# A four-layer block on one core: Delta net's gate moved from VectorE to ScalarE, the rope sum read from PSUM, and two chains of stages spread by one unit

## The reference, cut to what matters

```
q, k, v = x @ Wq, x @ Wk, x @ Wv
q, k = rope(q), rope(k)                      # u1*c - u2*s, u1*s + u2*c
q, k = elu(q) + 1, elu(k) + 1
beta = clip(sigmoid(x @ Wbeta + bbeta), 0.001, 0.999)
M = M * beta_t + k_t v_t^T ;  Z = Z * beta_t + k_t    # over the 1024 positions
y = (q_t M) / (q_t Z + eps)
```

## Time and profile before

| | |
|---|---|
| median of 3 runs | 1531.02 us (1529.54 to 1532.64) |
| profiled execution | 1541.69 us |
| its span | 1540.3 us |
| PE busy | 1185.7 us (77%) |
| DVE busy | 1129.7 us (73%) |
| ACT busy | 734.5 us (48%) |
| POOL busy | 704.0 us (46%) |
| mean granted clock of TensorE | 0.878 |

### The profile page before, as it was taken

One profiled execution on the slowest core, in us unless ns is written; L12 is line 12 of the kernel. 1 busy time (PEld: TensorE's weight loads), 2 busy tenths in 40 slices (PEclk: granted clock), 3 DMA queues, 4 the chain that ended last, 5 costly groups with the idle time before them and its releaser, 6 DMA issues.

```text
span 1540.3 us, 18685 instructions
## 1 busy us (share of the span) xinstructions
PE 1185.7 (77%) x5568; PEld 543.4 (35%) x5568; DVE 1129.7 (73%) x3003; ACT 734.5 (48%) x1599; POOL 704.0 (46%) x857
## 2 busy tenths in 40 slices
PE   3514986999998886657658678898989898988863
PEld 1212454555444443223222222333333333333322
DVE  5888645757988898578959786787888788876022
ACT  4634783255443253123230366656565656565641
POOL 7434672456777776438550122133412441335144
PEclk9856998999999996687875698999999999999995
DMA  3000104222111100004235101111020202000010
GB/s 107 0 1 0 46 1 108 80 77 62 35 48 42 35 14 0 0 4 63 43 51 78 20 1 30 32 17 35 4 33 15 37 4 33 4 1 3 1 42 14
DMA packets 33666, 47.02 MB, mean 31 GB/s; under 512 B 5007, under 2 KB 18191, under 8 KB 33263
## 3 DMA queue, kind: packets, MB, share of 16 engines
q1 hardware_dynamic: 30974, 43.84, 13.4%
q10 hardware_dynamic: 2592, 2.00, 0.5%
HBM read 39.14 MB, written 6.68 MB: 30 GB/s over the span
## 4 chain that ended last, share of the span: by engine, by line
PE 31%; DVE 21%; ACT 6%; issue 4%; POOL 4%; DMA 0%; ACTq 0%; DVEq 0%; POOLq 0%
PE PS L658 8%; PE PS L616 5%; PE PS L641 5%; DVE PS L1175 4%; DVE SS L1178 4%; PE PS L703 3%; DVE RB L1090 2%; PE PS L501 2%; PE PS L310 2%; ACT RB L1580 2%; DVE st L745 1%; ACT RB L1587 1%; DVE B L1090 1%; DVE PS L1070 1%; PE PS L520 1%
## 5 line engine op out<-in xcount | busy, mean ns | idle before, releaser
L1580 ACT ACTIVATE RB<-PS 128x512 f32<-128x512 f32 (+3 forms) x768 | 328.1, 497 | 265.7 <-PE PS L641 261.8
L616 PE MATMUL PS<-B 96*128 96x512 bf16 (+3 forms) x768 | 259.1, 360 | 55.6 <-DVE B L1221 24.2
L1829 POOL TENSOR_SCALAR_AFFINE_SELECT RB<-RB 128x512 f32<-128x512 f32 x128 | 81.3, 635 | 410.8 <-ACT RB L1580 410.8
L1175 DVE CUSTOM_DVE_ANT_0 PS<-PS,w_msk 128x128 f32<-128x128 f32 (+3 forms) x512 | 243.4, 503 | 29.1 <-PE PS L616 28.6
L641 PE MATMUL PS<-B 96*128 96x512 bf16 (+3 forms) x768 | 241.5, 336 | 18.6 <-ACT RB L1580 16.8
L1178 DVE TENSOR_REDUCE SS<-PS 128x1 f32<-128x512 f32 x256 | 175.2, 684 | 37.0 <-PE PS L616 36.1
L658 PE MATMUL PS<-RB,B 128*32 128x512 f32 (+3 forms) x1536 | 170.8, 517 | 14.4 <-ACT RB L1587 14.4
L616 PEld LDWEIGHTS PS<-B 96*128 96x128 bf16 x768 | 77.0, 101 | 204.8 <-DVE SS L1175 65.5
L1748 POOL TENSOR_TENSOR RB<-RB,B 128x512 f32<-128x512 f32 x64 | 82.6, 1292 | 92.9 <-DVE RB L983 68.1
L501 PE MATMUL PS<-B,WW 128*128 128x512 f32 x128 | 82.2, 776 | 37.6 <-DVE RB L1090 26.6
L641 PEld LDWEIGHTS PS<-B 96*128 96x128 bf16 x768 | 75.6, 100 | 99.1 <-ACT RB L1580 59.3
(11 more groups left out here) (243 smaller groups left out, 2229.3 us busy)
## 6 DMA issues: line engine op xcount, KB each, us to landing
B<-scrW SPq DMA_DIRECT2D x128, 128.0 KB, 3.0
B<-scrQ SPq DMA_DIRECT2D x72, 128.0 KB
scrQ<-B SPq DMA_DIRECT2D x6, 384.0 KB, 6.4
B<-scrK SPq DMA_DIRECT2D x36, 64.0 KB
X<-in_x SPq DMA_DIRECT2D x8, 256.0 KB, 8.5
out_dram<-X SPq DMA_DIRECT2D x8, 256.0 KB, 3.0
B<-in_w SPq DMA_DIRECT2D x3, 576.0 KB, 4.8
B<-in_zeros SPq DMA_DIRECT2D x9, 128.0 KB
```

The source lines that it names most:

```text
L616: pe.matmul(p[:, 0:w], qs[u % 3][:, h, 128 * i:128 * i + 128], keys_of(u, h)[:, 512 * c:512 * c + w], start=True, stop=True).then_inc(s["m ...
L1175: ins = dve.tensor_tensor_reduce(p, p, msk[:, 512 - w:512], 1.0, LOWEST, ALU.add, ALU.max, MX[:, u % 2, i, h, c:c + 1])
L1580: act.activation(RB[:, 4 * (step % 3) + z, 0:w], bank(bank_of["score", step, z])[:, 0:w], ACT.Exp).then_inc(s["ex2"], 1)
L1829: pool.affine_select(out=pb, in_=pb, compare_op=ALU.is_ge, fill=0.0, base=0, pattern=[[0, 4], [1, 128]], channel_multiplier=-1).then_inc(s ...
```

## The change

The gate 0.5 tanh + 0.5, clipped to 0.001..0.999, was two DVE operations on 128x512. It becomes three on ACT, each waiting for the one before: relu(0.5 t + 0.499), relu(0.998 - that), 0.999 - that. They stand in slices 12 and 13 ahead of the tanh of slice 12. The rope's second product is written back into its own PSUM bank, and the sum reads it there; the bank is lent until the sum is made. ACT's exp and relu go from slices 8, 10 to 9, 11 and DVE's elu from 9, 11 to 10, 12. `stats_m` goes from v-3 to v-4, `rstd` from v-4 to v-5, `add_m` and `add` from v-5 to v-6. POOL does what lies between units for the first unit of a step ahead of the product of the second.

```diff
@@ tensor_program, head_d
-                    banks.lend(i, s["t_d"], 4 * g + k - 6)
+                    w, half = divmod(k - 7, 2)
+                    if half:
+                        banks.lend(i, s["rot_d"], 2 * g + w + 1)
+                    else:
+                        banks.lend(i, s["t_d"], 4 * g + k - 6)
@@ vector_program, head_d
-                    dve.tensor_tensor(row(q + half), bank(bank_of["pj_d", g, k - 7]),
-                                      cs[:, half, 512 * h:512 * h + 512], ALU.mult).then_inc(s["t_d"], 1)
+                    p = bank(bank_of["pj_d", g, k - 7])
+                    dve.tensor_tensor(p if half else row(q), p, cs[:, half, 512 * h:512 * h + 512],
+                                      ALU.mult).then_inc(s["t_d"], 1)
                     if half:
                         dve.wait_ge(s["t_d"], 4 * g + k - 6)
-                        dve.tensor_tensor(row(q), row(q), row(q + 1), ALU.add).then_inc(s["rot_d"], 1)
-                if k in (9, 11):
-                    w = (k - 9) // 2
+                        dve.tensor_tensor(row(q), p, row(q), ALU.add).then_inc(s["rot_d"], 1)
+                if k in (10, 12):
+                    w = (k - 10) // 2
...
-                if k in (12, 13):
-                    d = BETA[k - 12][:, 512 * g:512 * g + 512]
-                    dve.wait_ge(s["beta_d"], 2 * g + k - 11)
-                    own.done(dve.tensor_scalar(d, d, 0.5, 0.5, ALU.mult, ALU.add))
-                    own.wait()
-                    dve.tensor_scalar(d, d, 0.001, 0.999, ALU.max, ALU.min).then_inc(s["gate_d"], 1)
@@ vector_program, between_m
-                if 0 <= v - 3 < 9 * NG and (v - 3) % 9 == 8:
-                    stats_m((v - 3) // 9)
+                if 0 <= v - 4 < 9 * NG and (v - 4) % 9 == 8:
+                    stats_m((v - 4) // 9)
@@ scalar_program, head_d
-                if k in (8, 10):
-                    w = (k - 8) // 2
+                if k in (9, 11):
+                    w = (k - 9) // 2
...
+                if k in (12, 13):
+                    d = BETA[k - 12][:, 512 * g:512 * g + 512]
+                    act.wait_ge(s["beta_d"], 2 * g + k - 11)
+                    own.done(act.activation(d, d, ACT.Relu, bias=FLOOR, scale=0.5))
+                    own.wait()
+                    own.done(act.activation(d, d, ACT.Relu, bias=SPAN, scale=-1.0))
+                    own.wait()
+                    act.activation(d, d, ACT.Copy, bias=0.999, scale=-1.0).then_inc(s["gate_d"], 1)
@@ scalar_program, between_m
-                if 0 <= v - 5 < 9 * NG and (v - 5) % 9 == 8:
-                    add_m((v - 5) // 9)
+                if 0 <= v - 6 < 9 * NG and (v - 6) % 9 == 8:
+                    add_m((v - 6) // 9)
@@ gpsimd_program, between_m
-                if 0 <= v - 4 < 9 * NG and (v - 4) % 9 == 8:
-                    rstd((v - 4) // 9, 1e-5, "m")
                 if 0 <= v - 5 < 9 * NG and (v - 5) % 9 == 8:
-                    g = (v - 5) // 9
+                    rstd((v - 5) // 9, 1e-5, "m")
+                if 0 <= v - 6 < 9 * NG and (v - 6) % 9 == 8:
+                    g = (v - 6) // 9
                     add(g, 8 + g + 1, rX[g % 2])
@@ gpsimd_program, the steps
                 if step < 36:
                     memory_c(step)
+                for v in beside(step)[0:1]:
+                    between_m(v)
                 for v in units[1:2]:
                     gated_m(v)
-                for v in beside(step):
+                for v in beside(step)[1:2]:
                     between_m(v)
```

More of the change, by code:

```diff
@@ L108, in build @@
         LN1W, LN1B, LN2W, LN2B, TS = [vecs[:, j:j + 1] for j in range(5)]
+        FLOOR, SPAN = vecs[:, 10:11], vecs[:, 11:12]
         ANW, FNW = vecs[:, 8:9], vecs[:, 9:10]
@@ L999, in head_d @@
                         dve.wait_ge(s["w_cs"], 16)
-                    dve.tensor_tensor(row(q + half), bank(bank_of["pj_d", g, k - 7]),
-                                      cs[:, half, 512 * h:512 * h + 512], ALU.mult).then_inc(s["t_d"], 1)
+                    p = bank(bank_of["pj_d", g, k - 7])
+                    dve.tensor_tensor(p if half else row(q), p, cs[:, half, 512 * h:512 * h + 512],
+                                      ALU.mult).then_inc(s["t_d"], 1)
                     if half:
                         dve.wait_ge(s["t_d"], 4 * g + k - 6)
-                        dve.tensor_tensor(row(q), row(q), row(q + 1), ALU.add).then_inc(s["rot_d"], 1)
-                if k in (9, 11):
-                    w = (k - 9) // 2
+                        dve.tensor_tensor(row(q), p, row(q), ALU.add).then_inc(s["rot_d"], 1)
+                if k in (10, 12):
+                    w = (k - 10) // 2
                     if g >= 6:
                         dve.wait_ge(s["sum_c"], ROWS_FROM)
-                    if k == 11:
+                    if w:
                         dve.wait_ge(s["so_m"], 16 * (range_of(g) + 1))
@@ L1983, in arrays @@
     cols = [L("ln1_w"), L("ln1_b"), L("ln2_w"), L("ln2_b"), L("time_shift").reshape(128), L("time_first"),
-            rep(bb[:, 0]), rep(bb[:, 1]), E("attn_norm_w"), E("ffn_norm_w")] + [z] * 6
+            rep(bb[:, 0]), rep(bb[:, 1]), E("attn_norm_w"), E("ffn_norm_w"), z + 0.499, z + 0.998] + [z] * 4
     D["vecs"] = np.stack(cols, axis=1)
```

## The result

The changed kernel takes 1552.22 us (median of 4 runs, 1551.07 to 1555.07) against 1531.83 (4 runs, 1529.54 to 1533.0): 1.0124 of the time before, 95% interval 1.0087 to 1.0161. It is slower by about 20 us, four times what was forecast, and above the range. The profiled execution took 1555.07 us, span 1553.1.

The account below looks back on a forecast made before the run. PE bounds units alone, PE and DVE fill batch 0, DVE leads batch 1, a chain sets batch 2. Terms 3.7 + 2.8 + 3.0 + 0 + 0 - 5.1 = +4.4, with +0.6 rounding +5: 1531.0 to 1536.0 us, range 1522 to 1547.

Parts of the forecast that it names:

- rival D: Two table loads of 1.28 us around each gate, on PE's path at units 28 and 34 to 36: 1541, chance 0.03.
- Unit 28 and the start: PE waits longer for ACT at unit 28 (+3.7) and the steps' start (+2.8); half speed behind these waits costs +3.0.
- Batch 0: 0: Steps at 366 to 465 us: DVE's wins and the new waits come out even, PE stays the bound; ends -4 and +4.
- Batch 1: 0: Steps at 465 to 582 us: waits against some 8 us of gates and 3.4 of rope sums, even; ends -5 and +5.
- Item (a): DVE's statistics of X in units 51 and 69 wait 6.3 us for POOL's add behind the memory; about 2 us elsewhere.
- Item (b): Slice 12: load, exp and relu ahead of slice 11's tanh make PE wait 2.5 us more, in groups 2 to 5.
- (c): Bank 7 is lent 0.7 us longer at slices 8 and 10.
- rival C: DVE's wait for X behind POOL's memory, units 51 and 69, twice 6.3 us on top of +5: 1548, chance 0.09.
- Batch 2: -5.1: 582 to 710 us: chain loses statistics, elu and gate time and waits, one elu comes in; ends -8 and -2.
- A: DVE's relief wins: batch 2's 5.1 us stays and batch 1 gives 4, so -9: 1522, chance 0.27.
- B: Gains and losses cancel: 1531, within 3; chance 0.22.
- E: No change in time, because DVE's and ACT's work both hide behind PE; counted within B.

Follow-up runs that it names:

- after: The changed kernel, with every part of the diff, against the kernel before: 1552.22 us, 1.0124 of before.
- before_again: The kernel before, unchanged, run once more for a second trace: 1532.35 us, span 1531.1 us.
- ln_alone: The kernel before with only the LayerNorm chain one unit later and POOL's order changed: 1555.66 us, 1.0141 of before.
- ln_early: The kernel before with the LayerNorm shift alone, POOL's between-unit work for a step's first unit ahead of its memory: 1538.27 us, 1.0005 of before.
- all_mended: The changed kernel with four orders moved: gate, exp and relu behind ACT's tanh, POOL's first unit ahead of memory, L1099/L1101 earlier on DVE: 1531.9 us, 0.9978 of before.
- gate_alone: The kernel before with the gate made by ACT, ahead of the tanh, and nothing else: 1538.03 us, 1.0035 of before.
- elu_alone: The kernel before with only exp and relu in slices 9 and 11 and elu in 10 and 12: 1558.42 us, 1.017 of before.
- rope_gate: The kernel before with the rope sum from PSUM and ACT's gate behind the tanh, LayerNorm and elu as before: 1524.27 us, 0.9929 of before.
- all_but_elu: The changed kernel with exp, relu and elu in their old slices: 1545.59 us, 1.0062 of before.

## Why the prediction was wrong

The sign was right, the size was not: 5 us were forecast, 20 came. The steps are taken here against the row "after" of the table. It sums to +22 us, 17 more than forecast: about 5 of them lie in batches 0 and 1, 3 at the start, 5 in batch 2 and up to step 30, and 5 in "early" and "rest", which tell nothing.

**What goes and what comes: right.** DVE lost 40.0 us, ACT gained 31.5 (34 forecast), the sum takes 0.69 us (0.7), no table load was added (rival D, 1541, is out). Over the rope sum the Trainium skill ("SBUF — State Buffer", Who interferes with whom) says that a VectorE instruction with two SBUF inputs contends with a GpSimd one that reads SBUF, and that one with a single SBUF input outside the 2-port modes does not; the trace agrees, 0.69 us in all 16 against up to 2.37 before. One reading of the prediction slipped: 1.8 us for a gate on DVE is less than 2.1 on ACT in the mean too, so the mean does not disagree with the rule that it stands beside.

**Unit 28 and the start: right in kind, a little short.** Predicted +3.7, +2.8 and 3.0 for the clock, 9.5; measured +12.1, of which 6.5 stand before the turn of unit 28 and 5.6 behind it. PE's timeline of after answers to the earlier trace rows:

```profile
343.11 0.63 PE L311 MATMUL PS<-w_ident,RB 128*128 128x128 f32 x4 [4.79 <-ACT SS L1466]
343.57 1.87 PE L429 MATMUL PS<-B,RB 128*128 128x128 f32 x8
345.24 1.91 PE L414 MATMUL PS<-B 128*128 128x512 f32 x2
346.94 1.07 PE L417 MATMUL PS<-B 128*128 128x512 f32 x2
...
375.97 0.66 PE L311 MATMUL PS<-w_ident,RB 128*128 128x128 f32 x4 [3.64 <-ACT RB L1308]
376.46 1.06 PE L429 MATMUL PS<-B,RB 128*128 128x128 f32 x8
```

The waits are 4.79 and 3.64 us (5.0 and 4.2 forecast), both on ACT as forecast. The clock cost two functions after the first, 0.8 + 0.9 = 1.7 us (2.0), and nothing after the second (1.0). Missing was the LayerNorm chain, of which I took no cost before the steps: alone it makes the start 3.6 us later; gate, elu and LayerNorm alone (+3.9, +3.1, +3.6) add to 10.6. It costs 2.9 us already 42 us before the turn of unit 28. ACT's scaling L1308, a unit later, waits 4.07 us for POOL's inverse root at 292.50, with silu behind it, so DVE's routing is late and PE waits for it:

```profile
301.30 0.60 PE L405 MATMUL PS<-w_ident,SS 128*16 128x128 f32 x4 [3.19 <-DVE SS L968]
```

In before_again this wait is 2.00 us; behind it L417 and L429 now take 1.85 and 1.91 us, where they took 1.02 and 1.05. ln_alone, ln_early and all_mended have the wait of 3.2 us, gate_alone, elu_alone and rope_gate that of 2.0.

**The step that failed: "Batch 0: 0" and "Batch 1: 0".** I listed most of the waits rightly. Item (a), the statistics of X of unit 51, in DVE's timeline of after (6.12 again at 584.65, unit 69), and POOL's ahead of it:

```profile
465.12 0.87 DVE L750 BATCH_NORM_STATS2 st<-X 128x6 f32<-128x128 f32 x4 [6.12 <-POOL X L1686]
```

```profile
459.08 2.35 POOL L1783 TENSOR_TENSOR SS<-B 128x1024 f32<-128x1024 f32 x1 [0.92 <-DVE B L1090]
461.51 2.36 POOL L1785 TENSOR_TENSOR SS<-SS,B 128x1024 f32<-128x1024 f32 x1
463.82 1.26 POOL L1686 TENSOR_TENSOR X<-X,RB 128x512 f32<-128x512 f32 x1
```

6.3 us were forecast, 6.12 came, twice, and 1.6 to 2.6 three times more. Item (b), PE's L462 in slice 12, waited 3.40 us for ACT's L1466 at 411.70 and 518.61 and ran at half speed behind it (1.93 and 2.08 us, 1.02 at full), in two groups and not in the four forecast. Exp and relu are not its only source: ACT's scaling ahead of them waits for POOL's inverse root, 6.03 us each time, and in all_but_elu, where exp and relu are a unit earlier, PE's wait is still 3.88 and 2.93 us. I had not listed this wait. ACT's row, then PE's:

```profile
406.34 1.65 ACT L1308 ACTIVATE RB<-RB,rs 128x128 f32<-128x128 f32 x4 [6.03 <-POOL rs L1660]
...
411.70 1.93 PE L462 MATMUL PS<-B,WW 128*128 128x512 f32 x2 [3.40 <-ACT B L1466]
```

What failed was the sentence that wins and waits "come out even", and in rival C the argument that PE still had work to do. The wins were there: rope_gate is 14.3 us shorter in batches 0 and 1, all_mended 10.4. After has +5.2. So the waits cost 16 to 20 us there (an estimate, the differences of these), where I let them do no more than cancel the wins. DVE's loss of 6 us is not covered by PE's queue of work: PE runs out of inputs from DVE within it (waits for L988 of 1.46 and 1.76 us at 466.9 and 471.5) and can pay again in clock, as the rows of ln_alone show. I also set the elu shift's price by item (b) and (c) alone; that L1012 moves in front of L1099, which frees bank 2, I did not follow, though it is in the same DVE loop.

**Batch 2: -5.1 forecast, -2.9 measured, and +2.7 given back by step 30.** The gates left the chain as said, and the elu stands in it with 0.68 and 0.67 us only. Most versions without DVE's gate give back 1.6 to 2.8 us before step 30 (after waits 5.44 us there for ACT's L1524 where before_again waited 4.55 for L1515). Why was not tested.

**The rest.** "Early" and "rest", +4.9 together, are within what two traces of one kernel differ by. The profiled execution of before was itself 9.2 us above its next trace: it was late before unit 28 (+6.4) and in batch 2 (+5.6), so the stretches I priced against were not typical ones either.

**The rivals.** C had the mechanism and nearly the time (1548): ln_alone's 22 us go with POOL's order. But they go with two waits, not with that for X alone, and in the whole change the LayerNorm shift taken out wins 4 to 9 us, so C is not the whole either. A (DVE's relief wins in the batches) is what happens without the two shifts and with the gate behind the tanh: rope_gate, 1524. B and E are out. Forecast and C are not alternatives; the loss of the start and the waits in the batches both came, and I gave the second 0.09 although its wait was in my own sum.

## What to carry to other kernels

When stages are moved by a unit, write down for each engine which instructions the moved one now stands behind and in front of, and who waits for those; a wait of 6 us on a nearly full engine was paid for the most part here, even though the engine behind it seemed to have work stored. Test a bundle of edits part by part: here two edits of little work (the rope sum and the gate behind the tanh) win 0.7%, and two "harmless" shifts cost 1.4 and 1.7% alone. Four changes of order undo this in the whole change; the elu shift alone, with its two orders mended, still cost 1.1%. Take a second trace of the kernel before before pricing stretches in it.

## What the runs showed of the hardware

A VectorE operation of one input (tensor_scalar, in place) took longer beside POOL as those of two inputs did: L1017 took 0.40 us free and 2.58 while POOL worked, L1019 0.43 and 2.47, against L1012 with 0.67 and 2.82 and L1004 with 0.69 and 2.37; with one operand in PSUM the sum never left 0.69. The Trainium skill ("SBUF — State Buffer", Who interferes with whom) has an operation like L1017, with one input in SBUF, among those that can hold the port shared with GpSimd; the trace agrees. After a wait of 3 to 5 us PE often ran its next two functions at half speed (L520 3.75 against 1.88 us, L462 1.93 against 1.02) and sometimes not (the turn at 375.97, after 3.64 us). In elu_alone the same L457 took 1.12 us at 411.64 and 2.08 at 522.55, each time after 3.01 us, so each wait has to be looked up. And one program's executions differ by 22 us (1527.5 to 1549.4 in 31 runs of before); some 5 us of it can arise in one stretch: batch 2 of before cost 5.6 us more in one trace than in the other.
